# Preparation moved into the norms, key parts reversed in DRAM and an unpaced scatter, in a four-layer kernel on one Trainium2 core

## The reference, cut to what matters

```python
xn = layernorm(x)
x = x + mixer(xn) + experts(xn)
```

```python
out = softmax(q @ k.T * 8 ** -0.5) @ v     # causal in layer 1
y = concat_heads(out) @ w_o + b_o
```

## Time and profile before

| | |
|---|---|
| median of 3 runs | 2041.15 us (2038.96 to 2044.38) |
| profiled execution, time | 2042.45 us |
| profiled execution, span | 2040.8 us |
| outside the span | 1.65 us |
| mean granted clock of TensorE, of full speed | 0.891 |
| PE busy | 1562.2 us (77%) |
| DVE busy | 1353.6 us (66%) |
| ACT busy | 1046.3 us (51%) |
| POOL busy | 822.6 us (40%) |
| DMA | 130.37 MB, 154089 packets, mean 64 GB/s |
| sections' starts | front 46.8, scan 185.9, norm1 821.8, att1 876.4, norm2 1388.0, att2 1408.4 us |

### The profile page before, as it was taken

How to read it: one execution, slowest core, us unless ns; L and a number is a source line. 1 busy time by engine, 2 the same in 40 slices (tenths; PEclk the granted TensorE clock), 3 DMA queues, 4 the chain that set the end, 5 groups by cost and what they waited for, 6 DMA issues and landing times. The chain is left out here.

```text
span 2040.8 us, 35899 instructions
## 1 busy us (share of the span) xinstructions
PE 1562.2 (77%) x12141; PEld 1067.5 (52%) x12143; DVE 1353.6 (66%) x2374; ACT 1046.3 (51%) x1858; POOL 822.6 (40%) x809
## 2 busy tenths in 40 slices
PE   4982888888866766546788889995499999649994
PEld 4761566556644444414566666662144444337883
DVE  7734778787799999575433338877772599536334
ACT  1464877887755544143433336662364577434440
POOL 3267555565598886067311114343310000024005
PEclk9995999999988878567899999996589999759997
DMA  3321011111000100544311113410541132111322
GB/s 126 102 66 56 28 50 55 31 47 50 16 24 25 30 24 8 201 150 132 81 42 44 44 40 79 91 48 25 155 90 56 38 65 50 53 49 41 99 67 78
DMA packets 154089, 130.37 MB, mean 64 GB/s; under 512 B 19697, under 2 KB 138632, under 8 KB 153682
## 3 DMA queue, kind: packets, MB, share of 16 engines
q1 hardware_dynamic: 141394, 104.58, 18.4%
q0 software_dynamic: 12544, 23.82, 4.1%
HBM read 77.08 MB, written 52.43 MB: 63 GB/s over the span
## 5 line engine op out<-in xcount | busy, mean ns | idle before, releaser
L666 POOL TENSOR_TENSOR xn_t<-xn_t,scan_du 128x512 f32<-128x512 f32 x256 | 320.8, 1268 | 176.7 <-ACT xn_t L808 101.0
L711 PE MATMUL banks<-scan_hc,ident 128*128 128x256 f32 x1024 | 297.2, 416 | 72.9 <-DVE scan_hc L863 72.9
L857 DVE TENSOR_TENSOR_SCAN xn_t<-banks,xn_t 128x512 f32<-128x512 f32 x256 | 311.5, 1217 | 42.1 <-ACT banks L798 35.9
L2274 ACT ACTIVATE att_pr<-banks 128x768 f32<-128x768 f32 (+1 forms) x256 | 234.4, 917 | 129.8 <-PE banks L2166 72.7
L798 ACT ACTIVATE banks<-delta,scan_exp_centre,a_neg 128x255 f32<-128x255 f32 x512 | 265.2, 559 | 45.8 <-DVE xn_t L857 45.5
L711 PEld LDWEIGHTS banks<-scan_hc,ident 128*128 128x128 f32 x1024 | 194.4, 209 | 136.2 <-DVE scan_hc L863 100.7
L863 DVE TENSOR_TENSOR scan_hc<-xn_t,banks 128x512 f32<-128x512 f32 x256 | 175.9, 687 | 25.9 <-PE banks L696 14.2
L917 POOL DMA_INDIRECT disp<-xn_tok,places x128 | 134.6, 1052 | 87.7 <-PE banks L395 45.5
L2318 DVE TENSOR_REDUCE att_mb<-banks 128x4 f32<-128x1024 f32 x128 | 153.9, 1222 | 21.3 <-PE banks L2133 16.4
L2182 PE MATMUL banks<-att_pr,att_vx 128*32 128x256 f32 (+1 forms) x2048 | 153.7, 373 | 4.8 <-ACT att_ot L2279 3.3
L1107 POOL IOTA route_rev<- 128x16 f32 (+2 forms) x3 | 0.4, 144 | 376.3 <-SPq L1123 310.4
(11 more groups left out here) (342 smaller groups left out, 3384.7 us busy)
## 6 DMA issues: line engine op xcount, KB each, us to landing
att_ks<-k_parts SPq DMA_DIRECT2D x384, 32.0 KB
scan_ew<-f_packed SPq DMA_DIRECT2D x12, 578.0 KB, 4.2
q_parts<-att_p_parts SPq DMA_DIRECT2D x16, 384.0 KB, 2.9
k_parts<-att_p_parts SPq DMA_DIRECT2D x16, 384.0 KB, 3.9
att_qs<-q_parts SPq DMA_DIRECT2D x64, 96.0 KB
gau_ew<-f_packed SPq DMA_DIRECT2D x8, 578.0 KB, 4.2
disp<-zeros SPq DMA_DIRECT2D x1, 4608.0 KB, 14.2
att_xin<-disp SPq DMA_DIRECT2D x72, 64.0 KB, 1.8
```

Source lines behind the costliest of these rows:

```text
L666: nc.gpsimd.tensor_tensor(bu[:, i % RING], b_sb[:, q % 2], du[:, b % 2, c:c + 1, :].to_broadcast([P, 2, T]), ALU.mult).then_inc(s.bu_made, 1)
L711: ins = nc.tensor.matmul(bank(Y_BANK)[:, c, :], g.ident[:], hc[:, i % RING, n, :], start=False, stop=(i % (PAIRS * DC) == PAIRS * DC - 1 a ...
L857: v.tensor_tensor_scan(rows(h[:, i % 2]), g.ps[:, DA + i % RING, :], rows(bu[:, i % RING]), 0.0, ALU.mult, ALU.add).then_inc(s.scan_done, 1)
L2274: nc.scalar.activation(pr[:, i % RING], g.ps[:, at:at + 2, 0:W], ACT.Exp, scale=scale).then_inc(s.p_ready, 1)
```

## The change

What it does, part by part:

1. `state_sel` becomes [96, 32]: one column per state. The matmuls take one column, repeated 128 times by a broadcast, as their stationary operand. The fill and the three selects work on 32 columns.
2. The router's bias and the convolution's bias are loaded in norm0, ahead of `w_in` and `w_taps`, and the front waits for them on a semaphore of their own.
3. The front's scatter has no pace.
4. `attention` opens its tiles and calls its norm (and in layer 1 the route) itself, through `prologue`. Its eight weight loads are issued in the norm, before the zeros of `disp`, and all its fills are POOL's `pool_job` there: in norm1 after the 32nd tile of `xn_tok`, in norm2 from the block's start. DVE no longer fills anything.
5. The parts of a chunk stand as six rows, queries high, middle, low and keys low, middle, high, so `k_parts` is reversed in DRAM and the keys of a half batch come in 3 DMAs instead of 6. Four buffers of parts in both sections; loads begin one chunk earlier (`EARLY` 2). ACT and DVE write the two parts of a kind through a strided view.
6. In att1 the bias `bo` is one DVE operation at the block's start; in att2 it stays 16 operations on POOL, after the last chunk of the projections. The scatter of att1 is issued whole from the block's start, without pace.
7. In `dense_experts` two tiles are declared earlier (memory only, not shown).

```diff
-                    pool_job(pool, s.job_done)
+                    pool_job(pool, s.xn_ready)
...
-
-                def pace(i):
-                    if i < 12:
-                        pool.wait_ge(s.xz_ready, AT_SCATTER + i // 2)
-                scatter(nc, pool, scattered, g.xn, disp, r, 2, pace=pace)
+                scatter(nc, pool, scattered, g.xn, disp, r, 2)
...
-        v = sel[2 * DS * q:2 * DS * (q + 1), :, :]
+        v = sel[2 * DS * q:2 * DS * (q + 1), :]
         nc.gpsimd.affine_select(out=v, in_=v, compare_op=ALU.not_equal, fill=1.0, base=0,
-                                pattern=[[-1, 2 * DS], [0, P]], channel_multiplier=1).then_inc(filled, 1)
+                                pattern=[[-1, 2 * DS]], channel_multiplier=1).then_inc(filled, 1)
...
+        def row(i):
+            return sel[:, i:i + 1].to_broadcast([3 * 2 * DS, P])
...
-                        ins = nc.tensor.matmul(bank(BO)[:, n, :], sel[:, 2 * pr + n, :], bc3[:, b * T:(b + 1) * T],
+                        ins = nc.tensor.matmul(bank(BO)[:, n, :], row(2 * pr + n), bc3[:, b * T:(b + 1) * T],
...
-                        ins = nc.tensor.matmul(bank(C_BANK)[:, n, :], sel[:, DS + 2 * pr + n, :],
+                        ins = nc.tensor.matmul(bank(C_BANK)[:, n, :], row(DS + 2 * pr + n),
...
+        if title == "route0":
+            dve.wait_ge(r.bias_in, 32)
...
+        def prologue(loads, fill):
+            with section(nc, "mixes", "mix_in0", "mix_in1") as mixes:
+                k = lora_buffers(mixes.sb)
+
+                def prefetch(sp):
+                    lora_loads(sp, t, k, mixes.sems)
+                    loads(sp)
+
+                def pool_job(pool, rows_done):
+                    pool.wait_ge(rows_done, NT)
+                    fill(pool)
+
+                normalise(nc, g, "norm1", g.x, g.xn, g.xn_t, router=t["f1_gate"], n_exp=E1, disp=disp, prefetch=prefetch,
+                          pool_job=pool_job)
...
-    EARLY = 3
-    w = sb("p_w", [P, 2, D])
-    b = sb("p_b", [P, 2])
+    EARLY, PB = 2, 4
...
-    parts = sb("p_parts", [P, PB, 3, 2, CH], BF16)
+    parts = sb("p_parts", [P, PB, 6, CH], BF16)
...
-                             parts[:, ch % PB, :, m]).then_inc(stored[ch % PB], 16)
+                             parts[:, ch % PB, 3 * m:3 * m + 3]).then_inc(stored[ch % PB], 16)
...
-            nc.vector.tensor_tensor(rem[:, ch % 2], y[:, ch % 2], parts[:, ch % PB, 0],
+            nc.vector.tensor_tensor(rem[:, ch % 2], y[:, ch % 2], parts[:, ch % PB, 0:6:5],
...
-            nc.vector.tensor_tensor(parts[:, ch % PB, 2], rem[:, ch % 2], parts[:, ch % PB, 1],
+            nc.vector.tensor_tensor(parts[:, ch % PB, 2:4], rem[:, ch % 2], parts[:, ch % PB, 1:5:3],
...
-            nc.scalar.copy(parts[:, ch % PB, 0], y[:, ch % 2]).then_inc(s.p_high, 1)
+            nc.scalar.copy(parts[:, ch % PB, 0:6:5], y[:, ch % 2]).then_inc(s.p_high, 1)
...
-            nc.scalar.copy(parts[:, ch % PB, 1], rem[:, ch % 2]).then_inc(s.p_mid, 1)
+            nc.scalar.copy(parts[:, ch % PB, 1:5:3], rem[:, ch % 2]).then_inc(s.p_mid, 1)
...
-    LOADS = 18 * 16
+    LOADS = 12 * 16
...
-    FILLS = 4
+    FILLS = BUFS + 3
...
+            for i in range(2):
+                sp.dma_start(p_w[:, i, :], project[2 * i]).then_inc(s.p_w_in, 16)
+                sp.dma_start(p_b[:, i:i + 1], project[2 * i + 1]).then_inc(s.p_w_in, 16)
+            for dst, src in ((bo_s, bo), (wv_s, wv), (wo_s, wo), (bv_s, bv)):
                 sp.dma_start(dst[:], src).then_inc(s.w_in, 16)
...
-            for row, part, n in ((0, 0, 3), (3, 0, 2), (5, 0, 1)):
+            for row, n in ((0, 3), (3, 2), (5, 1)):
                 sp.dma_start(qs[at + row * HD:at + (row + n) * HD, p], q_parts[
-                    part:part + n, :, tok].rearrange("a (d g j) t -> g (a d) j t", g=2, j=PAIRS)[half]
-                    ).then_inc(qk_in[p], 16)
-            for row, part, n in ((0, 0, 3), (3, 1, 2), (5, 2, 1)):
-                for i in range(n):
-                    sp.dma_start(ks[at + (row + i) * HD:at + (row + i + 1) * HD, p], k_parts[
-                        part, :, tok].rearrange("(d g j) t -> g d j t", g=2, j=PAIRS)[half]
-                        ).then_inc(qk_in[p], 16)
+                    0:n, :, tok].rearrange("a (d g j) t -> g (a d) j t", g=2, j=PAIRS)[half]).then_inc(qk_in[p], 16)
+                sp.dma_start(ks[at + row * HD:at + (row + n) * HD, p], k_parts[
+                    3 - n:3, :, tok].rearrange("a (d g j) t -> g (a d) j t", g=2, j=PAIRS)[half]).then_inc(qk_in[p], 16)
 
         def early_load(sp, b, half):
             sp.wait_ge(s.filled, FILLS)
...
-        def fill_beside(dve):
-            nc.vector.memset(ks[:, 2:4], -1.0).then_inc(s.filled, 1)
-            nc.vector.memset(mb[:], 0.0).then_inc(s.filled, 1)
-
         def fill(pool):
-            nc.gpsimd.memset(ks[:, 0:2], -1.0).then_inc(s.filled, 1)
-            nc.gpsimd.memset(vx[:], 0.0).then_inc(s.filled, 1)
+            for p in range(BUFS):
+                nc.gpsimd.memset(ks[:, p], -1.0).then_inc(s.filled, 1)
+            nc.gpsimd.memset(mb[:], 0.0).then_inc(s.filled, 1)
+            for p in range(2):
+                nc.gpsimd.memset(vx[:, p], 0.0).then_inc(s.filled, 1)
...
-            if moe:
-                scatter(nc, pool, r.scattered, g.xn, disp, r, 2, range(0, cut))
-            pool.wait_ge(s.w_in, 64)
-            for i in range(0, NT, 2):
-                nc.gpsimd.tensor_tensor(g.x[:, i:i + 2, :], g.x[:, i:i + 2, :],
-                                        bo_s[:, None, :].to_broadcast([P, 2, D]), ALU.add).then_inc(s.biased, 1)
+            pool.wait_ge(s.ones_set, 1)
+
+        prologue(weights, fill)
...
-                parts.weights(sp)
-                weights(sp)
...
-                fill(pool)
                 if dense:
+                    pool.wait_ge(s.p_low, NCH)
+                    for i in range(0, NT, 2):
+                        nc.gpsimd.tensor_tensor(g.x[:, i:i + 2, :], g.x[:, i:i + 2, :],
+                                                bo_s[:, None, :].to_broadcast([P, 2, D]), ALU.add).then_inc(s.biased, 1)
                     job.gpsimd(pool)
                 if moe:
-                    scatter(nc, pool, r.scattered, g.xn, disp, r, 2, range(cut, NT),
-                            lambda i: pool.wait_ge(s.m_ready, (i - cut) * 7 // 4 + 1))
+                    scatter(nc, pool, r.scattered, g.xn, disp, r, 2)
...
-                fill_beside(dve)
+                dve.wait_ge(s.w_in, 64)
+                if moe:
+                    v.tensor_tensor(g.x[:], g.x[:], bo_s[:, None, :].to_broadcast([P, NT, D]),
+                                    ALU.add).then_inc(s.biased, 1)
                 parts.vector(dve)
-                dve.wait_ge(s.w_in, 64)
-                dve.wait_ge(s.ones_set, 1)
...
-                            dve.wait_ge(s.biased, NT // 2)
+                            dve.wait_ge(s.biased, 1 if moe else NT // 2)
...
+    def prologue(loads, fill):
+        normalise(nc, g, "norm2", g.x, g.xn, g.xn_t, prefetch=loads, pool_job=lambda pool, rows_done: fill(pool))
...
-        sel = l.enter_context(nc.sbuf_tensor("state_sel", [3 * 2 * DS, 2 * DS, P], BF16))
+        sel = l.enter_context(nc.sbuf_tensor("state_sel", [3 * 2 * DS, 2 * DS], BF16))
...
+                sp.dma_start(r.bias[:], t["f0_router_b"].to_broadcast([P, E0])).then_inc(m.bias_in, 16)
+                sp.dma_start(f.bc[:], t["m_b_conv"]).then_inc(m.bias_in, 16)
                 sp.dma_start(f.w[:], t["m_w_in"]).then_inc(m.taps_in, 16)
                 sp.dma_start(f.wk[:], t["m_taps"].to_broadcast([P, TAPS, DI])).then_inc(m.taps_in, 16)
...
```

63 lines of the change are left out of this document (27 added, 36 removed).

## The result

On the first chip the changed kernel takes 2013.93 us, the median of 4 runs (2009.95 to 2014.23), against 2040.06 of the kernel before: ratio 0.9865, 95% interval 0.9844 to 0.9886. It is faster, by half of what was forecast, and lies outside the range of 1979 to 2009. The profiled execution took 2014.04 with a span of 2012.1. On two other chips the kernel before takes some 60 us more and the change makes it slower; that is told with the experiments.

A forecast was written before the change was run, and what follows sets the result against it. No resource was taken as near its bound over the whole span; gains lay in stretches where most engines stand still. Terms -5.8 - 16.3 + 0.7 - 16.2 - 17.0 = -54.6 gave span 1986.2, plus 1.65: 1988 us, range 1979 to 2009.

The forecast's parts named there:

- Norm0: Section norm0: three selects shrink to 32 columns, so L171 and L174 fall to 0.2 us each; -5.8 us.
- norm1: Section norm1: POOL does all fills after DVE's L186, ending at 853.6 against PE's end at 852.96; +0.7 us.
- small selection: The two matmuls whose weights become one repeated column: a weight load still takes 0.099 us; change 0.
- Front: Front: unpaced scatter starts near 70.9, issue ends near 162.0 with holds of 4.4 and 5.0, scan starts at 169.5; -16.3 us.
- Att1, up to the last store: Start of att1: first store at +11.85 from block start, chunks with a half batch at 4.7 us, last store at +37.4.
- Att2's: Att2 given att1's times: last store at +37.4, scores at +49.7 instead of +63.6; whole term with norm2 -17.0 us.
- The step that failed: Att1, last store to first score: 14.85 us falls to 12.8 through six key issues fewer; scores at +50.2.
- Batch 3 and the experts' first tile: Waits in the attentions shrink with fewer issues: batch 3's by 3.1 us in each, the first expert tile's by 2.1.
- Rival B: Attentions: DMA engines, not SP's issues, set the pace; 2007 us, chance 0.15.
- Rival C: Front: DVE holds the scatter, which keeps its 96.5 us; -10.9 instead of -16.3, 1993 us, chance 0.11.
- Rival D: Weight loads of `state_sel`: a repeated column loads slowly, making the kernel slower than before, up to 2111 us; chance 0.03.
- The slower side: Whole kernel measured slower than before the change; chance 0.03, against faster 0.95 and same 0.02.

## Why the prediction was wrong

- **Norm0, norm1, small selection:** right, each within 0.5 us, by the steps given.
- **Front:** the number is right within 0.4 us, in part by luck. Holds were taken at 9.4 us and came to 3.8, so the last issue ended some 5 us earlier than forecast; but then DVE's last operation was the limit instead of the scatter's landing, and gave as much back.
- **Att1, up to the last store:** right (+37.4 forecast, +37.3 measured), by two errors that cancel: the first store came 1.1 us earlier after PE's start, and the pace was 4.92 instead of 4.7. Att2's stands at +35.0, 2.4 us earlier than forecast, by a first store at 8.7 instead of 11.8, which other executions of the same code have at up to 11.7: luck again.
- **The step that failed:** "From it to the first score were 937.58 - 922.73 = 14.85, which hold the landing wait, load(2), then the maxima's transfer; six key issues fewer leave 12.8". The subtraction took the issues as the only term of that stretch that would move. What moved it was the transfers: the stores land 3.6 us later, and the rows take 1.3 us more; the issues themselves gave 1.1. Measured 18.6 and 17.4. With half of the packets it is 12.6: the sum was one of issues, the stretch one of packets. Why the landing got longer is shown in part. It took 7.9 us in att1 instead of 4.3; it takes 6.9 with six key issues and 7.0 with the loads a chunk later, so each of the two gives about 1 us; in att2, without a scatter, it took 7.4. The kernel with both undone was not run, and that the same packets stand in less time before the last store is argued, not shown.
- **Batch 3 and the experts' first tile** (-3.1 twice, -2.1): nearly nothing came (0.5, 0.6, -0.2), by the same mistake. With half of the packets att2's wait for batch 3 is gone; for the tile the place in the queue decides, and moving it cut the wait by 6.3 us.
- **What the 26 us are made of:** att1 gave 12.1 us less than forecast and att2 10.8. Of these the stretch behind the last store is 5.8 and 5.1, batch 3 2.6 and 2.4, the tile 2.3. The scan's 3.2 and the dip of the clock in att2, some 3, are not the change's. Without them the time would be about 2008 (an estimate, 2013.93 less the two), just inside the range; the step would be as wrong.
- **The row was there.** The window with 0.97 stood in the earlier trace rows, and I weighed it as 0.2 us on the pace. Rival B had the mechanism, and stood at 0.15 with 2007. Even so two of its terms were wrong: the pace did fall, from 5.52 to 4.92, and the stretch behind the last store did not stay as it was but got longer. It should have been given more than 0.15.
- **Rival C** (DVE holds the scatter) did not happen: the 64 issues took 85 us, not 96.5. One was held, for 3.1 us, and 62 took 1.06 us or less. **Rival D** did not: 0.099.
- The slower side came after all, and from a mechanism that was not among the rivals: on two chips the unpaced scatters nearly stop the other engines.

## What to carry to other kernels

Before an issue is counted as a saving, look at the DMA share of the stretch and of the one behind it. Here, at 0.97 and more, fewer issues gave some 2.6 us of a counted 5.3 at the first score. What helped was to put the transfer that someone waits for ahead of those that nobody needs yet (15.7 us, for a line moved). A pace that costs 17 us on one chip may save 20 to 30 on the next: try a change that takes one away on more than one chip.

## What was not expected of the hardware

- On two chips of the four or five used, indirect DMAs issued by POOL every 1.28 us let PE execute one instruction per 1.4 us, and DVE and ACT none for up to 60 us; the lag begins about 15 issues after the first. Chips with the stall took 2100.6 and 2102.6 for the kernel before, those without 2040 to 2043. With the front's pace it began at about 131 us instead of 83, again some 15 issues behind the last pause; with a drain every 16 issues it came all the same; with att1's pace the engines still lost 24.6 us, in small pieces. The kernel before took 60 us more on these chips as well. No profile of it there was taken; the kernel with both of its paces lost as much, in the front and in att1, which makes the same stall likely. The Trainium skill (SBUF — State Buffer, "SBUF: two separate sides") has PE and ACT never wait on the port pair that POOL and DVE share; here PE and ACT stood still as well, so that lock, as the page has it, does not explain it.
- Merging the DMAs made their packets take longer. One batch's loads and a little of the experts' input, 0.89 MB within 9 us, kept the DMA engines 0.55 busy with 18 issues and 0.75 with 12: about 41 and 57 ns of an engine for each packet (share x 16 x 9 us / packets). It goes with the merging and not with the rest of the change, since the changed kernel with six key issues is at 0.55 again. (Merged issues also follow each other faster, 4.8 us for a batch instead of 6.4, so form and density aren't told apart.) At the first score this did not make merging a loss, but it says that a high DMA share is not yet a high rate: the same bytes give 0.55 or 0.75. Rows of the kernel before, the changed one and the changed one with six key issues (queue, kind: packets, MB, share of 16 engines):

```profile
q1 hardware_dynamic: 1926, 0.89, 55.3%
```

```profile
q1 hardware_dynamic: 1895, 0.89, 75.0%
```

```profile
q1 hardware_dynamic: 1931, 0.89, 55.0%
```
